# A linear-attention layer feeding a graph of attention nodes: first-layer order of mean squares, values, next rows and statistics, scores by chunk, and another opening

## The reference

```
x = x + attn(layernorm(x))      # first layer
x = x + ffn(layernorm(x))       # graph of six attention nodes

attn(x): h = rms(x) * w
  q, k, v = h@Wq, h@Wk, h@Wv            # 64, 64, 128 wide, 4 heads
  glog = log_sigmoid(h@Wgk1@Wgk2 + b) / 16
  b = cumsum(glog) within chunks of 64 tokens
  A = tril((q exp(b) scale) @ (k exp(-b))^T)    # inside a chunk
  o = A @ v + (q exp(b) scale) @ S;  S carried from chunk to chunk
  o = rms(o per head) * silu(h@Wg);  x2 = o@Wo + x
  return x2 + (silu(n@W_gate) * (n@W_up)) @ W_down,  n = rms(x2)
ffn: six nodes; node c is act_w[c]*mha(q,k,v) + q, where q, k, v are
  earlier nodes times edge weights We, times ew[c]; 8 heads, softmax over
  the 256 tokens of a sequence; a layer norm with gain and bias at the end
```

## Time and profile before

| what | us |
|---|---|
| median of 3 runs | 1013.59 |
| the runs | 1010.59 to 1014.52 |
| the profiled execution, its own time | 1014.45 |
| its span, first to last instruction | 1012.6 |
| PE, DVE, ACT, POOL busy | 967.2, 837.4, 691.1, 453.5 |
| mean granted TensorE clock | 0.981 |

### The profile page before, as it was taken

The page is one execution under the profiler, slowest core; times in us unless marked ns, Lnnn a source line. Parts: engine busy times, 40 slices in busy tenths (PEclk is TensorE's granted clock), DMA queues, the critical chain, the costliest instruction groups (busy, mean ns, idle before and its releaser), DMA issues.

```text
span 1012.6 us, 26339 instructions
## 1 busy us (share of the span) xinstructions
PE 967.2 (96%) x9513; PEld 684.0 (68%) x9513; DVE 837.4 (83%) x1879; ACT 691.1 (68%) x1520; POOL 453.5 (45%) x883
## 2 busy tenths in 40 slices
PE   7989999998899999999999999999999999999995
PEld 4665555665567777777777777777777777777763
DVE  4475777766689988998998999999898988988996
ACT  3345666665377777777677678788777677777775
POOL 4522222224343443444544446666634435534455
PEclk9789999999899999999999999999999999999998
DMA  9100000001334434434434344444434444344321
GB/s 227 48 1 0 1 0 0 0 1 42 126 128 154 144 129 156 142 129 158 140 130 167 129 139 165 139 140 165 148 128 163 136 139 160 128 151 148 128 97 34
DMA packets 109526, 112.86 MB, mean 111 GB/s; under 512 B 23354, under 2 KB 83518, under 8 KB 109406
## 3 DMA queue, kind: packets, MB, share of 16 engines
q1 hardware_dynamic: 108478, 111.09, 32.7%
q0 software_dynamic: 128, 0.14, 0.2%
q10 hardware_dynamic: 800, 0.05, 0.1%
HBM read 6.90 MB, written 2.10 MB: 9 GB/s over the span
## 4 chain that ended last, share of the span: by engine, by line
PE 80%; DVE 10%; ACT 4%; issue 3%; POOL 1%; DMA 0%; DVEq 0%; SPq 0%; ACTq 0%; POOLq 0%
PE bank L1331 80%; DVE region L1189 1%; DVE region L1121 1%; DVE region L1011 1%; ACT region L857 1%; DVE region L1116 1%; ACT region L833 1%; DVE region L1109 1%; DVE region L976 1%; ACT region L727 1%; ACT L833 0%; DVE region L1102 0%; ACT region L800 0%; DVE region L1041 0%; ACT region L802 0%
## 5 line engine op out<-in xcount | busy, mean ns | idle before, releaser
L1189 DVE TENSOR_REDUCE region<-bank 128x2 f32<-128x512 f32 x768 | 493.8, 675 | 67.8 <-PE bank L1331 57.5
L857 ACT ACTIVATE region<-bank 128x512 f32<-128x512 f32 x768 | 406.4, 600 | 175.5 <-PE bank L1331 165.1
L1331 PE MATMUL bank<-st 64*128 64x256 f32 x3072 | 311.1, 326 | 6.5 <-DVE region L1189 5.3
L1331 PEld LDWEIGHTS bank<-st 64*128 64x128 f32 x3072 | 245.4, 192 | 21.9 <-DVE region L1189 7.4
L1331 PE MATMUL bank<-region 128*32 128x256 f32 (+3 forms) x3554 | 250.0, 377 | 1.7 <-ACT region L857 0.7
L1331 PEld LDWEIGHTS bank<-region 128*32 128x32 f32 (+2 forms) x3554 | 130.6, 117 | 84.7 <-issue 15.8
L631 POOL TENSOR_TENSOR mxp<-region,one_col 128x16 bf16<-128x16 f32 x96 | 20.8, 217 | 338.8 <-DVE region L1189 338.8
L1331 PE MATMUL bank<-mst,ones 64*128 64x512 bf16 x768 | 150.9, 387 | 0.5 <-ACT region L857 0.2
L612 POOL TENSOR_TENSOR hl<-qk,hl 128x512 fp32r<-128x512 f32 x96 | 122.5, 1276 | 7.5
L609 POOL TENSOR_TENSOR hl<-qk,one_col 128x512 fp32r<-128x512 f32 x96 | 99.9, 1040 | 10.1 <-ACT qk L822 9.9
L1331 PEld LDWEIGHTS bank<-mst,ones 64*128 64x128 bf16 x768 | 37.3, 93 | 85.0 <-issue 38.6
(11 more groups left out here) (194 smaller groups left out, 1225.4 us busy)
## 6 DMA issues: line engine op xcount, KB each, us to landing
st<-hl SPq DMA_DIRECT2D x384, 256.0 KB, 2.6
mst<-mrows SPq DMA_DIRECT2D x384, 4.0 KB
out<-xall SPq DMA_DIRECT2D x14, 128.0 KB, 2.5
xall<-in_L_attn_hidden_states SPq DMA_DIRECT2D x1, 768.0 KB, 7.9
cst<-in_constants SPq DMA_DIRECT2D x1, 514.5 KB, 4.2
xT<-in_L_ffn_Wq SPq DMA_DIRECT2D x1, 384.0 KB
xT<-in_L_ffn_Wk SPq DMA_DIRECT2D x1, 384.0 KB
xT<-in_L_ffn_Wv SPq DMA_DIRECT2D x1, 384.0 KB
```

What stands on the lines that cost most here:

```text
L857: act.activation(to, x_bank(x, k, e)[:, :].rearrange("p (j q) -> p j q", j=2), ACT.Exp).then_inc(B["exp_ok"], 1)
L1189: dve.tensor_reduce(mx[s.n % 2][:, to:to + 2], s_bank(s, k, e)[:, :].rearrange("p (j k) -> p j k", j=2), AX_X, ALU.max, negate=True).then_ ...
L1331: return pe.matmul(o, w, x, start=start, stop=stop, skip_group_check=skip)
```

## The change

POOL's fills of `mst` and `mxp` move from the very start to the end of `stack_heads`, the fills of `qbd`, `keT` and `kvs` come before the four transfers, and the fill of `am` waits for `wa_ok` (the first layer's scaled weights). On DVE a slot begins with the statistics of the next group and, from slot 3 on, the root and the rows of the later norm, and only then come `uu` and `qke`. In slots 0 and 1 the last two score copies stand ahead of the state updates, and the last fold and the biases move to the end of slot 1. On PE the mean squares stand ahead of v; the last fold products stand behind the outputs of slot 1; a score tile is two products, one for each chunk of 64 tokens, each onto its own 64 output rows; the warm products before z are 3, 11 and 12 in slots -1, 0 and 1 (3 each before), and those before q and k are left in slot 0 alone.

```diff
@@ POOL, start
-            for n in range(2):
-                pool.memset(mst[n][:, :, :], 0.0).then_inc(S["ones_ok"], 1)
-            for n in range(2):
-                pool.memset(mxp[n][:, :, :, MPARTS, :], 0.0).then_inc(S["pads_ok"], 1)
-            (the four pool.dma_start of scal and lng)
             pool.memset(eps_col[:, :], RMS_EPS).then_inc(S["eps_ok"], 1)
             pool.memset(one_col[:, :], 1.0).then_inc(S["one_ok"], 1)
             pool.memset(qbd, 0.0).then_inc(S["pads_ok"], 1)
             pool.memset(keT, 0.0).then_inc(S["pads_ok"], 1)
             pool.memset(kvs, 0.0).then_inc(S["pads_ok"], 1)
+            (the four pool.dma_start of scal and lng)
+            pool.wait_ge(S["wa_ok"], 1)
             pool.memset(am, 0.0).then_inc(S["am0"], 1)
@@ POOL, end of stack_heads
+                for n in range(2):
+                    pool.memset(mst[n][:, :, :], 0.0).then_inc(S["ones_ok"], 1)
+                    pool.memset(mxp[n][:, :, :, MPARTS, :], 0.0).then_inc(S["ones_ok"], 1)
@@ DVE, first: the order at its start is now
                 e = late(j)
                 if f is not None:   # bn_stats of f
+                if e is not None:
+                    newton(dve, ve3, rr3, rt3, e, "r3a", "r3b", "r3c", "rstd3_ok")
+                    dve.wait_ge(A["rstd3_ok"].sem, A["rstd3_ok"].at(e))
+                    x1_rows(e)
                 if k is not None:   # uu
                 if i is not None:   # qke
@@ DVE, further down
-                if isinstance(i, int) and i == 1:
-                    scale_fold(4)
-                    scale_fold(5)
-                    biases()
-                (newton and x1_rows of e)
+                opening = isinstance(i, int) and i < 2
+                if opening:
+                    scores(i, 2)
+                    scores(i, 3)
                 if i is not None:   # kvs, sg
...
-                if i is not None:
+                if i is not None and not opening:
                     scores(i, 2)
                     scores(i, 3)
... (end of first)
+                if isinstance(i, int) and i == 1:
+                    scale_fold(4)
+                    scale_fold(5)
+                    biases()
@@ PE, first
-                if isinstance(i, int) and i == 1:
-                    fold_products(4)
-                    fold_products(5)
-                    for c in range(NODES):
-                        n = mm(bank[6][:, 64 + c:65 + c], wo_raw[:, c, :], bprod[:, c, 2:3])
-                    n.then_inc(S["bo_ps"].sem, 1)
-                    pe.wait_ge(S["fold_ok"], 5)
+                if isinstance(i, int) and i == 2:
+                    pe.wait_ge(S["fold_ok"], NODES)
...
-                        warm(3)
+                        warm((3, 11, 12)[f])
... (after the outputs o)
-                    if isinstance(f, int) and f in (1, 2):
+                    if isinstance(f, int) and f == 1:
                         warm(3)
+                    if isinstance(i, int) and i == 1:
+                        pe.wait_ge(A["am_ok"], TPI * i + TPI)
+                        fold_products(4)
+                        fold_products(5)
+                        (the six products with bprod)
                     mm(bank[2][:, :], wa[:, 0:2 * QK], hT).then_inc(A["qkp_ps"], 1)
+                if f is None and i is not None:
+                    warm(6, 3)
+                if i is not None:
+                    pe.wait_ge(A["sq_ok"].sem, A["sq_ok"].at(i))
+                    if k is not None:
+                        pe.wait_ge(A["nT_ok"], k + 1)
+                    mm(bank[5][:, :], mean_dv, sq).then_inc(A["ms_ps"].sem, 1)
+                if f is not None:   # v of f, then as before b of f
@@ PE, heads_scores
-                mm(bank[[4, 1][t % 2]][:, :].rearrange("p (h c) -> p h c", h=GH), qke[:, t * P:(t + 1) * P],
-                   qbd[:, :, t * P:(t + 1) * P]).then_inc(a_ps[t], 1)
+                for c in range(P // CHUNK):
+                    own, at = slice(c * CHUNK, (c + 1) * CHUNK), t * P + c * CHUNK
+                    n = mm(bank[[4, 1][t % 2]][own, :].rearrange("p (h c) -> p h c", h=GH)[:, :, own], qke[:, at:at + CHUNK],
+                           qbd[:, :, at:at + CHUNK])
+                n.then_inc(a_ps[t], 1)
```

More of the change, by code:

```diff
@@ L938, in first @@
             def first(f, i, k, j):
-                if k is not None:
-                    dve.wait_ge(A["t1_ok"], k + 1)
-                    dve.wait_ge(A["rstd_ok"].sem, A["rstd_ok"].at(k))
-                    dve.tensor_tensor(uu, osb, sq, ALU.mult).then_inc(A["u_ok"].sem, 1)
-                if i is not None:
-                    dve.wait_ge(A["eb_ok"], i + 1)
-                    dve.wait_ge(A["qkp_ps"], i + 1)
-                    dve.tensor_tensor(qke, bank[2][:, :], eb, ALU.mult).then_inc(A["qke_ok"], 1)
                 e = late(j)
@@ L957, in first @@
                     n.then_inc(A["bn1"].sem, 1)
+                if e is not None:
[3 more added lines that the diff above has]
+                if k is not None:
+                    dve.wait_ge(A["t1_ok"], k + 1)
+                    dve.wait_ge(A["rstd_ok"].sem, A["rstd_ok"].at(k))
+                    dve.tensor_tensor(uu, osb, sq, ALU.mult).then_inc(A["u_ok"].sem, 1)
+                if i is not None:
+                    dve.wait_ge(A["eb_ok"], i + 1)
+                    dve.wait_ge(A["qkp_ps"], i + 1)
+                    dve.tensor_tensor(qke, bank[2][:, :], eb, ALU.mult).then_inc(A["qke_ok"], 1)
                 if f is not None:
@@ L965, in first @@
                     dve.tensor_tensor(x2, quads(5), xn, ALU.add).then_inc(A["x2_ok"].sem, 1)
-                if isinstance(i, int) and i == 1:
-                    scale_fold(4)
-                    scale_fold(5)
-                    biases()
-                if e is not None:
-                    newton(dve, ve3, rr3, rt3, e, "r3a", "r3b", "r3c", "rstd3_ok")
                 if f is not None:
@@ L977, in first @@
                     dve.tensor_scalar(ve[:, 1, :], mv[:, :, 1], 1.0 + RMS_EPS, RMS_EPS * LN_EPS, ALU.mult, ALU.add).then_inc(A["ve_ok"].sem, 1)
-                if e is not None:
-                    dve.wait_ge(A["rstd3_ok"].sem, A["rstd3_ok"].at(e))
-                    x1_rows(e)
                 draining = f is None and i is None
@@ L1468, in first @@
                 if f is not None:
-                    if isinstance(f, int) and f in (1, 2):
+                    if isinstance(f, int) and f == 1:
                         warm(3)
+                    if isinstance(i, int) and i == 1:
+                        pe.wait_ge(A["am_ok"], TPI * i + TPI)
+                        fold_products(4)
+                        fold_products(5)
+                        for c in range(NODES):
+                            n = mm(bank[6][:, 64 + c:65 + c], wo_raw[:, c, :], bprod[:, c, 2:3])
+                        n.then_inc(S["bo_ps"].sem, 1)
                     if i is None:
@@ L1473, in first @@
                     mm(bank[2][:, :], wa[:, 0:2 * QK], hT).then_inc(A["qkp_ps"], 1)
+                if f is None and i is not None:
+                    warm(6, 3)
+                if i is not None:
+                    pe.wait_ge(A["sq_ok"].sem, A["sq_ok"].at(i))
+                    if k is not None:
+                        pe.wait_ge(A["nT_ok"], k + 1)
+                    mm(bank[5][:, :], mean_dv, sq).then_inc(A["ms_ps"].sem, 1)
+                if f is not None:
                     for t in range(TPI):
@@ L1482, in first @@
                     fold_transposes(1)
-                if f is None and i is not None:
-                    warm(6, 3)
-                if i is not None:
-                    pe.wait_ge(A["sq_ok"].sem, A["sq_ok"].at(i))
-                    if k is not None:
-                        pe.wait_ge(A["nT_ok"], k + 1)
-                    mm(bank[5][:, :], mean_dv, sq).then_inc(A["ms_ps"].sem, 1)
                 if f is not None:
```

18 lines of the change are left out of this document (9 added, 9 removed).

## The result

The changed kernel takes 1007.04 us (median of 6 executions, 1006.74 to 1007.09); the kernel before, run on the same chip, 1012.13 (6 executions, 1010.41 to 1016.14). The ratio is 0.9937, 95% interval 0.9916 to 0.9957: faster, by 0.4 to 0.8%. The forecast was 1001.5 with a range to 1008. The sign and the range held, the range by 1 us; the size did not. The profiled execution of the changed kernel took 1007.08, 7.4 less than the profiled one of before, with a span of 1005.3 (1012.6), a mean granted clock of 0.986 (0.981) and PE busy 955.5 us (967.2).

The account below looks back on a forecast made before the run. It took a chain of waits as the bound, with PE standing and falling to half clock in the opening slots. Terms 4.0 + 4.3 + 3.0 + 0.4 + 0.5 + 0.7 = 12.9 off 1014.45 gave 1001.5 us, range 996.5 to 1008.

Parts of the forecast that it names:

- the prediction's own signs of being wrong: Clock of 0.50 in either opening slot, loop slot over 26.3 or under 25.7 us, or DVE wait for x before first qke.
- first loop pass: Slot 2 to slot 3, counted among loop slots 3 to 6: -0.1 us, like each of the four.
- (b): Rival: statistics and later rows ahead of uu make uu 0.7 us later in six slots; 1005.7 us, chance 0.09.
- Opening: Start to z's first reader: moved POOL fills free DVE's L976 and ACT's root, PE keeps full clock; -4.0 us.
- rival (c): Opening: POOL's fills are not what held L976, so the opening gives nothing; 1005.5 us, chance 0.08.
- Slot 0: z to first fold product: earlier scores, halved tiles and warm products start the fold at 42.15 instead of 46.4; -4.3 us.
- rival (a): Slot 0 or 1: clock falls in the stand before the carried state, giving back 3 to 4 us; 1005 us, chance 0.15.
- Slots 1 and 2: Forecast as slot 1: qke at 77.35 against 84.66, a further -3.0 us; bounds 0 to -4.
- Loop passes 4 to 6: Loop slots: ms earlier, but small steps wait for POOL's product and uu comes when it came; -0.1 us each.
- Slots 7 and 8: Slot 7: shorter DVE wait behind two score tiles, -0.5; slot 8: later rows go into the root's wait, -0.7 us.
- Halved tiles: Score tiles: halves on different output rows overlap, 0.4 us per tile; the skill's tiling-mode drain rule stood against it.
- Rival (d): Loop slots: halved tiles and earlier later-norm rows empty PE, clock falls, +4 us in six slots; 1025 us, chance 0.04.

Follow-up runs that it names:

- experiment 4: Kernel before with only the changed POOL opening (fills and transfers reordered, waits adapted): median 1007.78 us, ratio 0.996.
- experiment 1: Changed kernel with the product that last_bias copies moved on PE ahead of q and k of slot 2: median 1004.52 us, ratio 0.9918.
- experiment 6: Changed kernel with 3 warm products in slots 0 and 1 instead of 11 and 12: median 1013.55 us, ratio 1.0002.
- experiment 7: Changed kernel with DVE's old order, uu and qke ahead of statistics and later rows: median 1006.93 us, ratio 0.9942.
- experiment 10: Changed kernel with v ahead of the mean squares again on PE: one execution, 1009.2 us.
- experiment 11: Changed kernel with experiment 1's edit, ACT's later-norm root ahead of o's square and copy, DVE's small steps and rows ahead of statistics: median 1006.13 us, ratio 0.9932.
- experiment 2: Changed kernel with whole score tiles again, one product of 512 columns per 128 tokens: median 1010.04 us, ratio 0.9977.
- experiment 3: Changed kernel with 7 warm products before the state-chain wait in slot 0 and 8 before uu's reader in slot 1: median 1008.44 us, ratio 0.995.
- experiment 8: Changed kernel with experiment 1's edit and warm products in PE stands from slot 0 on: median 1001.66 us, ratio 0.99.
- experiment 9: Experiment 8 with 4 warm products instead of 8 before uu, and statistics and later rows behind uu and qke up to slot 6: median 1001.56 us, ratio 0.988.
- experiment 12: Kernel before, unchanged, run again for a second trace: one execution, 1009.63 us.

## Why the prediction was right and wrong

The number lay in the range, but two of the prediction's own signs of being wrong came: a clock of 0.50 in both opening slots, and a loop slot over 26.3 us (28.65). The first fold product came at 40.4 and not near 38. That 1007.0 still lay under 1008 owes something to luck, for the largest single miss, the first loop pass, stood in the sum at -0.1, and no rival but (b) touched it, with 0.7.

**Opening: right.** -3.86 for -4.0; what POOL did ahead of its last fill held L976, and rival (c) is out (experiment 4, which moves fills and transfers together). The rows end at 9.8 as forecast, z's first reader follows 2.54 us later (2.5 forecast), and the clock stays up.

**Slot 0: the mechanism wrong, -2.16 for -4.3.** The prediction read the chain's 10.7 us at the end of the slot as a property of the kernel; the second trace of before shows that it is one of two outcomes. The path that it worked out was nearly right as it stands (z's first reader to the fold in 25.9 us, 26.40 measured with the clock up); the length of before from which it took the gain was not the kernel's. And it priced PE's stand before the carried state as harmless, from a stand of 1.4 us in slot 8 that left the clock at 1.00. Here the stand was 1.67 us and the clock fell 0.7 us after its end. This is rival (a), and its chance of 0.15 was far too low. Of seven traces with this stand at 1.66 or 1.67 us six have a fall that begins in it or up to 2.1 us behind it (the changed kernel's two and experiments 1, 6, 7, 10; experiment 6 has a second stand, of 1.36 us, just ahead) and one has not (experiment 11, with 39.24 - 12.84 = 26.40 to the fold); one with 1.51 has not (experiment 2), nor have the three with it filled (3, 8, 9). Before, the stand of 2.29 us went with the fall in one trace and not in the other, nor in experiment 4. It costs 1.65 us in the changed kernel and 3.2 at most (29.55 in experiment 7), where (a) gave it 3 to 4.

**Slots 1 and 2: -1.89 for -3.0.** The falls of the changed kernel, at 49.4 to 56.2 and at 83.5, take the difference; its second trace, without the one at 83.5 and with 3.4 us instead of 6.8 in the first, gave -2.9. The uncovered statistics cost the 0.8 that the prediction had counted (experiment 7). They cost more than it had counted: they lengthen PE's stand before `uu`'s reader from 0.96 to 1.73 us, and in all seven traces with that stand the clock falls in it or up to 0.8 us behind it, in none of the four with 0.96 us (before, its second trace, experiments 4 and 7). As in slot 0, the gain is one of clock: all three traces with the old code here (with experiment 4) have a fall of 10 us that begins in the stand of 2.6 us before z, which the twelve warm products fill; and experiment 6, with that fall back and two short ones, took 62.47 us for this stretch against 59.73 before.

**First loop pass: the step that failed outright, +2.37 for -0.1.** The prediction gave the same -0.1 to each of "four slots". But the first pass does not start like the others: `last_bias` stands between slot 2 and the loop, and its copy on DVE waits for a product that PE makes behind b. The prediction moved the statistics and the rows "ahead of `uu`" and asked what covers them; it did not ask what stands ahead of them. The cover it counted on, DVE's wait for the root, was already used up by another wait. Taking only that wait away gives 2.6 us back (experiments 1, 8), and so does putting `uu` back in front (2.3, experiment 7). A prediction by this case's rows could have had it: the copy and the `uu` behind it stand in the trace of before, 0.33 us apart.

**Loop passes 4 to 6: right in size, and in what holds `uu`.** -0.12 for -0.1. `uu` comes 4.03 us behind the square of o (4.05 before), "when it came", with the port as the reason. Where the 0.12 then come from no run shows; the prediction took its 0.1 without a sum, so that the size agrees is partly luck. And the new order is no gain here: the old one makes the passes 0.21 shorter (experiment 7). The small step's 1.00 us up to the end of POOL's product, against 0.16 when it is free (experiment 11), agrees with the rule of the Trainium skill (SBUF — State Buffer, "Who interferes with whom") that the prediction named, and so do the rows of experiment 11: that section counts tensor_scalar among the operations that can take the shared pair, and the four rows took 2.18 us beside POOL's product and 1.12 clear of it. So the 0.4 us that the small steps' release would give by the rule, as the prediction worked it out, is not to be had by release alone; what comes free first meets the next user of the port. Rival (b), 0.7 per slot, did not happen at that size in the loop, though in the first pass the moved work did hold `uu` up, by 2.6.

**Slots 7 and 8: right, -1.78 for -1.2.** The later rows ahead give 0.9 (experiment 7), the halved tiles 0.5 (experiment 2); no run shows what gives the other 0.4.

**Halved tiles: right.** They overlap, and the drain by the Trainium skill (TensorEngine Tiling (Array Packing), "Key Properties") has no visible price here: passes of 26.01 to 26.02 with and without. Rival (d) did not happen. There is a fall in slot 3 in the changed kernel's second trace (104.6 to 108.0) and in experiments 2 and 3 (110.7, 109.1), each 0.1 to 0.5 us behind the stand of 1.8 us in which PE waits for the late `uu`, with whole tiles too, and none where that stand is gone (experiments 1, 7, 8, 9, 11) or in a later pass:

```profile
105.66 1.16 PE L1334 MATMUL bank<-wo,region 128*128 128x128 f32 x8 [1.81 <-DVE region L957]
```

The line is of the changed kernel's first trace, where the clock stayed up behind it.

**Still open.** In experiments 3, 8 and 9 the clock falls at 47.7 to 47.9 us while the records show PE at work: 0.1 to 0.3 us after the warm products before `uu`'s reader have begun, behind a stand of 0.27 us and fold products of one column and of 128 columns in turn (in the changed kernel 2.00 of 2.00 us busy from 45 to 47, at 1.00). Filling that stand of 1.73 us so did not hold the clock, while with the stand at 0.96 us it stayed up behind the same fold products (experiment 7). No experiment took these products out, so their part in it isn't shown. Nor is it known why in some executions a given stand goes with a fall and in others not, nor whether the whole tiles of experiment 2 draw a longer one. The changed kernel's executions near 1012 us (clock 0.983) were not traced. And experiment 9's first layer is shorter than that of experiment 8 by 1.7 us in the two traces (235.15 against 236.87 at POOL's product; 1.1 of it in slot 1 and 3 x 0.21 in the passes), while the medians, from different chips, are 0.1 apart.

## What to carry to other kernels

When work is moved into a wait, look on the engine's own stream for every instruction between the new place and that wait, in the straight-line slots that enter and leave a loop as well as in the loop: a wait of 3.4 us ahead of the moved work took away its cover and cost 2.4 us once, more than 0.1 us per pass could give. A slow stretch in one trace is not yet a property of the kernel: before its removal is counted as a gain, look whether a second trace has it. Where PE's clock falls, fill the stands of that stage together and not only the one that the trace shows, then judge by stretches with their clock in more than one trace; with the stands filled and the bias's product early (experiment 8) the kernel is 5 us faster than the changed one. An edit can be worth nothing beside another (ms ahead of v: 0.01 us per pass with the new order on DVE, up to 0.33 with the old one), so each is to be tried without the other.

## What the runs showed of the hardware that was not expected

- Two executions of the same program can differ by 5 us, 4.4 of them through one fall of the clock: the kernel before with and without a fall in slot 0 (stretch to the fold 30.21 and 25.80 us).
- The warm products decide more than the order of the real ones: with 8 and 9 of them fewer in slots 0 and 1 the kernel took 7.1 us more.
- One and the same stand of 1.67 us went with a fall of the clock in six traces and not in a seventh; the stand of 2.29 us of the kernel before did in one trace and not in two others (experiments 4 and 12). With the stand of 1.67 us filled there was no fall in three traces. A stand raises the risk of a fall here, it doesn't decide it.
- The clock fell in three traces with PE at work by the records (experiments 3, 8, 9, at 47.7 to 47.9 us).
- The four rows on DVE beside a POOL product of 1.27 us took 2.18 us instead of 1.12.
